# Another ending, four tiles of squares summed by TensorE, and new places for the interleaved work

## What is computed

```
x = x + mixer(layernorm(x))     # selective scan, 8 heads, state 64 x 128
x = x + ffn(layernorm(x))
x = x + attention(layernorm(x)) # 16 heads of width 8; its sequence axis is the batch of 8
x = x + ffn(layernorm(x))

# mixer, for each step t of 512
h = alpha * h + beta * Bx_prev + gamma * Bx_t
y_t = h . C_t
y = rmsnorm(y);  return y @ out_proj_w.T
```

## Time and profile before

| | us |
|---|---|
| median of 3 runs | 598.55 (597.16 to 598.97) |
| the profiled execution | 597.6 |
| its span, first to last instruction | 595.8 |
| busy: PE, DVE, ACT, POOL | 521.4, 470.9, 479.9, 433.6 |
| mean granted clock of PE | 0.968 |
| first scan, last scan start | 45.2, 523.9 |

### The profile page before, as it was taken

One profiled execution on the slowest core, in us unless ns is written; L12 is line 12 of the kernel. 1 busy time (PEld: TensorE's weight loads), 2 busy tenths in 40 slices (PEclk: granted clock), 3 DMA queues, 4 the chain that ended last, 5 costly groups with the idle time before them and its releaser, 6 DMA issues. The chain is left out here.

```text
span 595.8 us, 12817 instructions
## 1 busy us (share of the span) xinstructions
PE 521.4 (88%) x3932; PEld 435.3 (73%) x3932; DVE 470.9 (79%) x1093; ACT 479.9 (81%) x1477; POOL 433.6 (73%) x568
## 2 busy tenths in 40 slices
PE   4979999999999889899999898999999787879187
PEld 4867888888887777688887777788777665756085
DVE  5665577677767999997758999997559999954994
ACT  3799999999998987789998869699999889853101
POOL 7447777888778696977778786877768886954742
PEclk9989999999999999999999999999999999998669
DMA  8832122222111111133211121232211211000001
GB/s 191 234 101 64 59 77 98 60 81 89 49 59 61 60 50 35 61 95 96 60 38 59 61 61 54 66 96 95 72 50 39 69 62 65 21 19 2 0 1 36
DMA packets 52302, 39.35 MB, mean 66 GB/s; under 512 B 7302, under 2 KB 48011, under 8 KB 52235
## 3 DMA queue, kind: packets, MB, share of 16 engines
q1 hardware_dynamic: 45898, 35.39, 20.2%
q10 hardware_dynamic: 6336, 3.15, 1.8%
HBM read 33.44 MB, written 4.46 MB: 64 GB/s over the span
## 5 line engine op out<-in xcount | busy, mean ns | idle before, releaser
L937 ACT ACTIVATE turned<-ps,sct 128x128 f32<-128x128 f32 x376 | 110.2, 446 | 0.0
L922 ACT ACTIVATE turned<-ps,sct 128x128 f32<-128x128 f32 x368 | 102.9, 433 | 5.1 <-issue 4.3
L1282 DVE TENSOR_TENSOR_SCAN lmat<-arow,band 128x512 f32<-128x512 f32 x64 | 86.0, 1349 | 3.6 <-POOL band L651 3.6
L630 POOL TENSOR_TENSOR cn<-turned 128x256 f32<-128x256 f32 x64 | 54.9, 858 | 39.9 <-ACT turned L937 39.9
L1816 PE MATMUL ps<-cT,bT 128*128 128x128 f32 x512 | 71.4, 283 | 8.6 <-DVE state L1321 6.3
L1290 DVE TENSOR_TENSOR mmat<-ps,lmat 128x512 f32<-128x512 f32 x64 | 43.9, 686 | 44.0 <-PE ps L1816 43.8
L1816 PEld LDWEIGHTS ps<-cT,bT 128*128 128x128 f32 x512 | 64.1, 193 | 15.7 <-issue 14.5
L630 POOL TENSOR_TENSOR bn<-turned 128x256 f32<-128x256 f32 x64 | 51.9, 811 | 28.5 <-PE ps L1848 16.9
L828 ACT ACTIVATE area<-ps 128x256 f32<-128x256 f32 (+1 forms) x68 | 34.8, 568 | 39.9 <-PE ps L2049 14.3
L1721 PE MATMUL ps<-w_sel_hi,xt_hi 128*128 128x512 f32 x128 | 59.5, 465 | 1.6 <-ACT turned L937 1.6
L1848 PE MATMUL ps<-wu,bn 128*128 128x128 f32 x384 | 53.7, 283 | 3.5 <-DVE mmat L1290 3.4
(11 more groups left out here) (272 smaller groups left out, 1408.3 us busy)
## 6 DMA issues: line engine op xcount, KB each, us to landing
arow<-alpha_rows SPq DMA_DIRECT2D x32, 512.0 KB, 3.8
drow<-decay_rows SPq DMA_DIRECT2D x64, 128.0 KB, 3.0
area<-in_L_attn_a_x_dram SPq DMA_DIRECT2D x4, 512.0 KB, 6.6
xT_rows<-turned SPq DMA_DIRECT2D x4, 512.0 KB, 5.4
xt<-xT_rows SPq DMA_DIRECT2D x32, 64.0 KB, 2.5
area<-in_L_attn_a_x_dram ACTq DMA_DIRECT2D x6, 256.0 KB, 3.1
out_dram<-area ACTq DMA_DIRECT2D x6, 256.0 KB, 2.5
area<-L_attn_a_sel_proj_w_dram SPq DMA_DIRECT2D x2, 512.0 KB, 6.8
```

Of the source, the lines that this page charges most:

```text
L630: pool.tensor_tensor(out[:, 0], zc[:, 0], zs[:, 1], ALU.subtract)
L922: last = act.activation(dst[h][:, N * q:N * q + N], bank(BK_B)[:, N * q:N * q + N], ACT.Copy, scale=scalars(c, k)[:, at + HH * h + q:at + ...
L937: last = act.activation(dst[h][:, N * q:N * q + N], bank(BK_C)[:, N * q:N * q + N], ACT.Copy, scale=scalars(c, k)[:, at + HH * h + q:at + ...
L1282: dve.tensor_tensor_scan(lmat[h], arow[i2][:, HH * P * h:HH * P * (h + 1)], band[h], 0.0, ALU.mult, ALU.add).then_inc(l_dve, 1)
```

## The change

- **Squares.** For tiles 3 to 6 of every chunk `y_square` writes the squares in place order, `y_sum` is left out, and `project_out` sums the four blocks by four products with the column of ones into one bank column, where it was one product. `ysq` has two buffers now, by the tile's parity.
- **Places and orders.** All positions of `PLACE` are new, and so are the orders of `step` on POOL, ACT, DVE and PE.
- **Values.** `f_hvals` also writes the values with the row inside, (h, d, r), to `vals_er`, which lies in the buffer of chunk 2's x; so it waits for that chunk's stores. Rows 4 to 7 are weighed in this layout, and DVE sums the 8 rows of each by a reduction (`sum_values`); PE then only transposes them (`turn_row`). Rows 2 and 3 are folded from 8 blocks to 4 on POOL. Rows 0 and 1 stay.
- **Warming.** PE turns the identity ahead of the last tile's `project_out` (after y and after its squares), at three points ahead of the first values' sums (8 turns each), once between rows 0 and 1, and 8 turns in each of pairs 2 and 3.
- **Banks and order in the tail.** Pairs have other PSUM banks for their outputs, so the biases go in earlier. `attended` and `norm_of` alternate, and pairs 2 and 3 are turned and multiplied one after the other.

The diff, cut:

```diff
+SQUARES_ON_PE = (3, 4, 5, 6)
+def sums_done(c, b):
+    return (NB - len(SQUARES_ON_PE)) * c + len([q for q in range(b + 1) if q not in SQUARES_ON_PE])
...
-        ysq = sb("ysq", [P, 4 * P])
+        ysq_both = sb("ysq", [P, 2, 4 * P])
...
+        vals_er = area[:, 3072:4096].rearrange("p (e r) -> p e r", r=NB)
...
-        o_bank = [bank(BK_C), bank(BK_Y), bank(BK_C), bank(BK_Y)]
-        ffn_bank = [bank(BK_F0), bank(BK_M), bank(BK_F1), bank(BK_T)]
+        o_bank = [bank(BK_C), bank(BK_Y), bank(BK_F0), bank(BK_M)]
+        ffn_bank = [bank(BK_C), bank(BK_Y), bank(BK_F1), bank(BK_T)]
...
-                elif k < 0:
+                else:
                     scalars_ready(pool, c, k)
...
                     if ok(k, 1):
-                        band_of(c, k)
-                    at_span(pieces, c, k, 0, 0.583, first)
...
+                    if ok(k + 1, 1):
+                        band_of(c, k + 1)
...
+            def fold(s):
+                pool.wait_ge(tg, TG["v", s])
+                tick(pool.tensor_tensor(wide[s][:, 0:512], wide[s][:, 0:512], wide[s][:, 512:1024], ALU.add), ("a", s))
             values_of(2)
+            fold(2)
             values_of(3)
+            fold(3)
...
             def y_square(c, b):
-                after(act, q_dve, tile)
-                act.activation(ysq[:].rearrange("p (t j) -> p j t", j=4), yT[b % 2].rearrange("p (j t) -> p j t", j=4), ACT.Square)
+                after(act, o_pe, tile - 1)
+                own = ysq_both[:, b % 2]
+                if b in SQUARES_ON_PE:
+                    act.activation(own, yT[b % 2], ACT.Square).then_inc(ysq_act, 1)
+                else:
+                    act.activation(own.rearrange("p (t j) -> p j t", j=4), yT[b % 2].rearrange("p (j t) -> p j t", j=4),
+                                   ACT.Square).then_inc(ysq_act, 1)
...
             def f_hvals(c, p):
+                evac(vals_last[:, pair(p), :], rows)
+                for g in range(2):
+                    act.wait_ge(rows_free[g], 16 * NC)
+                evac(vals_er[:, :, pair(p)].rearrange("p e s -> p s e"), rows).then_inc(ha[p], 1)
...
             def y_sum(c, b):
+                if b in SQUARES_ON_PE:
+                    return
...
+            def sum_values(s):
+                if s in (4, 5):
+                    dve.wait_ge(tg, TG["v", s])
+                else:
+                    dve.wait_ge(tv, TV["v", s])
+                end_tick(dve.tensor_reduce(xn[:, s], wide[s].rearrange("p (e r) -> p e r", r=NB), AX.X, ALU.add), ("r", s))
...
             values_of(6)
             values_of(7)
-            fold(6, 512, "v", "a")
-            fold(7, 512, "v", "a")
-            fold(6, 256, "a", "h")
-            fold(7, 256, "a", "h")
+            sum_values(4)
+            sum_values(5)
+            sum_values(6)
             attended(0)
+            sum_values(7)
             attended(1)
             norm_of(0)
+            attended(2)
             norm_of(1)
-            attended(2)
             attended(3)
+            norm_of(2)
             add_to_x(0, ffn_bank[0], "F", "af")
             add_to_x(1, ffn_bank[1], "F", "af")
-            norm_of(2)
             norm_of(3)
...
             def project_out(c, b, more):
+                if in_ending(c) and b == NB - 1:
+                    for signal, count in ((y_dve, UNITS * NC), (ysq_act, NT)):
+                        pe.wait_ge(signal, count)
+                        keep_warm(WARM_LAST, BK_T)
...
+                if b in SQUARES_ON_PE:
+                    for j in range(4):
+                        last = pe.matmul(bank(BK_M)[:, D:D + 1], ysq_both[:, b % 2, P * j:P * j + P], ones[:, 0:1], start=(j == 0), stop=(j == 3))
...
+            for name in ("sum", "rec", "w"):
+                pe.wait_ge(tv, TV[name, 0])
+                keep_warm(WARM_VALUES, BK_C)
             add_rows(0, 0, NB)
+            pe.wait_ge(tv, TV["sub", 1])
+            keep_warm(WARM_LAST, BK_C)
             end_tick(add_rows(0, 1, NB), ("acc", 0))
-            add_rows(1, 2, NB)
-            end_tick(add_rows(1, 3, NB), ("acc", 1))
+            add_rows(1, 2, NB // 2)
+            end_tick(add_rows(1, 3, NB // 2), ("acc", 1))
...
-            add_rows(2, 4, NB)
-            end_tick(add_rows(2, 5, NB), ("acc", 2))
-            add_rows(3, 6, 2)
-            end_tick(add_rows(3, 7, 2), ("acc", 3))
+            for p in (2, 3):
+                turn_row(p, 2 * p)
+                keep_warm(WARM_ROWS, BK_T)
+                end_tick(turn_row(p, 2 * p + 1), ("acc", p))
+                out_of(p)
```

More of the change, by code:

```diff
@@ L1018, in f_hvals @@
                 act.wait_ge(hp[p], HEAD_P["KV"])
[L1019 removed]
+                rows = kv_bank[p].rearrange("p (s e) -> p s e", s=2)[:, :, D:2 * D]
+                evac(vals_last[:, pair(p), :], rows)
+                for g in range(2):
+                    act.wait_ge(rows_free[g], 16 * NC)
+                evac(vals_er[:, :, pair(p)].rearrange("p e s -> p s e"), rows).then_inc(ha[p], 1)
             def f_hrow(c, p):
@@ L1141, in _ @@
             exp_of(1)
-            turned_out("acc", 0, 0)
-            turned_out("acc", 1, 0)
-            turned_out("acc", 2, 0)
-            turned_out("acc", 3, 0)
+            for p in range(4):
+                turned_out("acc", p, 0)
             for p in range(4):
@@ L1858, in project_out @@
                     pe.matmul(bank(BK_M)[:, 0:D], yT[b % 2][:, P * j:P * j + P], w_out[:, j], start=(j == 0), stop=(j == 3))
-                pe.matmul(bank(BK_M)[:, D:D + 1], ysum[:], ones[:, 0:1], start=True, stop=True).then_inc(o_pe, 1)
+                if b in SQUARES_ON_PE:
+                    for j in range(4):
+                        last = pe.matmul(bank(BK_M)[:, D:D + 1], ysq_both[:, b % 2, P * j:P * j + P], ones[:, 0:1], start=(j == 0), stop=(j == 3))
+                else:
+                    last = pe.matmul(bank(BK_M)[:, D:D + 1], ysum[:], ones[:, 0:1], start=True, stop=True)
+                last.then_inc(o_pe, 1)
             def f_free(c, use):
@@ L1992, in step @@
                         project_b(c, k + 2)
-                    at_span(pieces, c, k, 0.45, 0.65, first)
                     if ok(k):
                         scores(c, k)
-                    at_span(pieces, c, k, 0.65, 0.75, first)
+                    at_span(pieces, c, k, 0.375, 0.542, first)
                     if ok(k + 2, 1):
                         project_c(c, k + 2)
-                    at_span(pieces, c, k, 0.75, 0.9, first)
+                    at_span(pieces, c, k, 0.542, 0.75, first)
                     if ok(k + 1):
                         turn_b(c, k + 1)
-                    at_span(pieces, c, k, 0.9, 1, first)
+                    at_span(pieces, c, k, 0.75, 0.833, first)
+                    if ok(k):
+                        outputs(c, k, not first or k >= FIRST_INTER)
+                    at_span(pieces, c, k, 0.833, 1, first)
                 else:
@@ L2005, in step @@
                         states(c, k - 1)
-                    if ok(k - 1):
-                        outputs(c, k - 1, not first or k - 1 >= FIRST_INTER)
-                    at_span(pieces, c, k, 0, 0.158, first)
                     if ok(k):
                         turn_c(c, k)
-                    at_span(pieces, c, k, 0.158, 0.263, first)
+                    at_span(pieces, c, k, 0, 0.147, first)
+                    if ok(k - 3):
+                        project_out(c, (k - 3) // 2, not (last and (k - 3) // 2 >= NB - 2))
+                    at_span(pieces, c, k, 0.147, 0.529, first)
                     if ok(k + 2, 1):
                         project_b(c, k + 2)
-                    at_span(pieces, c, k, 0.263, 0.316, first)
-                    if ok(k - 3):
-                        project_out(c, (k - 3) // 2, not (last and (k - 3) // 2 >= NB - 2))
-                    at_span(pieces, c, k, 0.316, 0.868, first)
+                    at_span(pieces, c, k, 0.529, 0.618, first)
                     if ok(k):
                         scores(c, k)
-                    at_span(pieces, c, k, 0.868, 0.921, first)
+                    at_span(pieces, c, k, 0.618, 0.824, first)
                     if ok(k + 2, 1):
                         project_c(c, k + 2)
+                    at_span(pieces, c, k, 0.824, 0.882, first)
                     if ok(k + 1):
                         turn_b(c, k + 1)
-                    at_span(pieces, c, k, 0.921, 1, first)
+                    at_span(pieces, c, k, 0.882, 1, first)
             def operands_ready():
@@ L2101, in _ @@
             ffn_of(1)
-            turn_pair(2)
-            turn_pair(3)
-            ffn_of(2)
-            ffn_of(3)
+            for p in (2, 3):
+                turn_pair(p)
+                ffn_of(p)
 _INS = ["L0_attn_a_x", "L0_attn_a_in_proj_w", "L0_attn_a_sel_proj_w", "L0_attn_a_out_proj_w", "L0_attn_a_A_log",
```

188 lines of the change are left out of this document (96 added, 92 removed), and 69 rows, old and new, of tables (PLACE, TV).

## The result

The changed kernel takes 607.75 us in the median (605.44 to 609.54), before 598.69 beside it: 1.016 of it, 95% interval 1.0127 to 1.0193. The forecast was 585.0 us, in 577.5 to 593.5. The profiled execution of the changed kernel is its fastest, 605.44 us (span 603.7); the span grew by 7.9 us.

The account below looks back on a forecast made before the run. ACT paced chunk 0, DVE the attention stage, PE and ACT units 14-15, waits the ending. Gains 5.4 + 1.0 + 0 + 0 + 5 + 2 = 13.4 us took 597.6 to 584.2, median 585.0 us; range 577.5 to 593.5.

Parts of the forecast that it names:

- the squares: Loop: sums of tiles 3 to 6 leave DVE and ACT writes squares plainly; 5.4 + 1.0 us won.
- the ending: After the last scan, some 72 us: head 5 us and tail 2 us won.
- the order: Loop: each engine's new step order is nearly the old one, cut elsewhere; 0 us, bounds -5 and +4.
- What bounds the kernel: Chunk 0: ACT, PE just behind; units 6 to 13 from chunk 1: DVE; units 14 and 15: PE and ACT.
- ACT's 1.0 us: Unit 14 of chunks 1 and 2: plainly written squares save ACT 2 x 0.5 us.
- 9 x 0.60: Chunks 1 to 3, where DVE is full: nine DVE sums removed, 0.60 us each, 5.4 us won.
- the cover: PE's side: 6 more passes per tile cost 0.65 us, fitting PE's free 1.5 us in the attention stage.
- Chunk 0, taken as 0: Chunk 0's four pairs: PE rises to some 12.2 us, ACT falls to 11.4; 0 us, bounds -2.0 and +1.4.
- The head: Start of the ending: last pair's norm 3.6 us sooner, idle 2.9 us gone, less costs; 5 us won, bounds 0 and 7.
- The tail: Last scores to last add: DVE's chain replaces PE's passes, with warming and POOL folds; 2 us won, bounds -1 and 4.
- PE as the pace: Rival: PE paces every tile, 10.4 us added and the loop's 6.4 not shown; 602 us, chance 0.05.
- Orders and places win by themselves: Rival: new orders and places fill DVE's idle time around the attention; 580 us, chance 0.16.

Follow-up runs that it names:

- a1: The kernel before with only the squares of tiles 3 to 6 summed on PE: 601.92 us, ratio 1.004 to 1.011.
- a4: The changed kernel with no squares on PE, all tiles summed by DVE: 610.73 us, ratio 1.017 to 1.025.
- a3: The kernel before with squares on PE and the new ending, old orders and places: 598.30 us, ratio 0.998 to 1.003.
- a2: The kernel before with the new ending alone, old orders and places, no squares on PE: 593.52 us, ratio 0.992 to 0.996.
- e1: Kernel before with the new ending alone, plus 12 PE turns ahead of unit 11's scores in chunks 1 and 2: 595.08 us, ratio 0.991 to 0.997.
- f1: Kernel before with new ending, PE squares only for tiles 3 to 5 of chunks 1 to 3, 8 turns before unit 11's scores (chunks 1, 2); repeat run: 594.01 us.
- e2: The kernel before with the new ending but without its new warming turns: 598.95 us, ratio 0.998 to 1.003.
- b4: The changed kernel with DVE's y_sum moved back behind the weighing of scores: 608.86 us, ratio 1.013 to 1.022.
- b2: The changed kernel with the old places for the head's pieces only: 604.42 us, ratio 1.007 to 1.015.

## Why the prediction was wrong

By the medians the 22.7 us between forecast and result are three sizes: the squares 11.2 (6.4 to win, 4.8 lost), orders and places 9.5, the ending 3.3 (7 forecast, 3.7 won); their sum of 24.0 is over by about what the kernel before was faster on the chip of a1 to a4 (597.26 for 598.69). With the order at its 0 the kernel would still have been outside the range, at a3's 598.3; the order made it slower than before.

**What bounds the kernel** was read rightly stage by stage, but units 14-15 too lightly. "The pair of units 14 and 15 is bound by PE and ACT together" stood there, and in the sum I let ACT's 1.0 us count there and forgot PE's passes.

**The squares**, 5.4 + 1.0 + 0 forecast, measured 0 between single profiled loops without a fall, and 4.8 us lost in the median of a3 against a2. Two steps failed. The first is the 9 x 0.60: six of the nine sums gave 0.1 to 0.9 us a pair and three gave 0.0 to 0.1, since the scan behind them met a POOL sum and took 0.55 longer; by pairs of e1 and f1 some 3.2 us are won for the 5.4. The second is the cover. Passes were costed where DVE is full; those of the later tiles land in units 14 to 1, where PE is nearly full, and e1 to f1 give 3.3 us back in units 14-15. Chunk 0, taken as 0, lost 0.7 us in units 12-13 (12.11 in a3 for 11.38), where PE was the pace. The plain square was right, 0.63 us. The loss in the median beyond that stays open: it is there at equal mean clock, and the one profiled execution of a3 is its fastest.

**The order**, "I take 0, bounds -5 and +4", measured +9.5 (a3 to the changed kernel), and is the step by which the kernel came out slower than before. No bound from rows stood behind +4: it was 0.15 us for each of 30 pairs, a guess. Inside it: x_high 2.0 us in chunk 0's pairs, a wait for a load in front of ACT's work where ACT sets the pace, of which I had named the move and not asked when the load lands; the head's places 3.3 us by the medians; y_sum 0 in this order; PE's outputs at most a gain, 2.4 us by the medians. The rest, some 6 us, is argued and not shown: by elimination it lies with the attention's places and cuts.

**The head**, 5 us forecast, measured 1.0: from the last scan to the last scores 32.9 us (535.0 to 567.84), 33.8 before (523.9 to 557.77). The wait for pair 2's add went, 3.6 us, as worked out. But 2.9 came ahead of it, between the last scan and the last output. Behind the last pair's first norm only 0.2 was won, for the 2.9 of the idle time before 550.66: 2.0 went as DVE's second norm met the POOL product that had been moved ahead. Of that product I counted the gain and not whom it shuts out, though I did so for the fold. And a2, with the old places, is at its last scores 31.5 us after its last scan (523.9 to 555.35), less than the changed kernel's 32.9: the earlier pieces bought nothing that the new ending with the old places did not.

**The tail**, 2 us forecast, measured 2.2: last scores to last add 33.6 us (567.84 to 601.45), 35.8 before. DVE's subtraction beside POOL's second product was held for 0.6 (0.4 taken). But I put the gain down to DVE's chain in place of PE's; e2 shows that without the turns nothing of it is left (36.2 us in its tail; 34.4 in a2).

**The rivals.** Slower than before had 0.04 and one mechanism, PE as the pace, which alone had 0.05: the chances did not agree. "Orders and places win by themselves" had 0.16, and its mirror image, that they lose, none, though bounds of -5 and +4 allow both.

## What to carry to other kernels

A table of places that was made for one order of steps says nothing under another: an order and its places are one change, and where no row prices them their range has two sides of at least the size of their stages. An edit that relieves the engine that sets the pace of one stage has to be followed with its work into the next stage, and work pulled into a full loop from an ending with idle time is paid at the loop's price. The largest new wait in a profile need not cost anything: b4 took 27 us of it away and gained nothing, while three waits of 0.45 to 0.8 us in front of ACT, where it sets the pace, cost 2.0. An instruction taken off a full engine pays only if the next one doesn't start into a neighbour's lock (the scan of 1.76 us for 1.21). And one profiled execution of a kernel is one draw: a late load or a fall of the clock in it is no property of the change until it shows in others.

## What the runs showed of the hardware

PE's low clock came in the middle of the loop too. In seven kernels (before, changed, a1 to a4, b2) there were sixteen falls in chunks 1 to 3: each began beside or within 2.3 us behind a pause of PE of 1.2 to 3.5 us, and PE then ran at 0.50 for 3.4 to 6.8 us. A pause need not bring one: the same seven executions have 75 pauses of 1.15 us and more there, and b4's has 14, up to 2.60 us, without a fall. With twelve turns in each of the two pauses of 2.0 us e1 had no fall, where five of six such pauses without turns had one. A fall of 3.4 us cost 0.8 us where DVE was the full engine (a2 to e1). The Trainium skill's "TensorE: Matmul & The Clock Gate" (The two states you'll see) calls the low clock the default that activity releases; the trace agrees, and shows that it can cost a full loop too.

Two DVE tensor_scalar instructions of 128x128 took 2.63 us together, 0.61 five us before: the second ran 2.37 us for 0.34, beside a POOL product of 2.37 us that had started 0.08 us ahead of it. The Trainium skill's "SBUF — State Buffer" (Who interferes with whom) names tensor_scalar among the VectorE operations that can shut GpSimd out and be shut out by it for a whole instruction, and says that a reduction never is; the trace agrees in the one, and DVE's row sums of the tail (1.2 us each, beside POOL's products) in the other.

A DVE scan took 1.76 us for 1.21 when it started 0.25 us behind a POOL sum of 0.92 us (f1 and e1, once in each of chunks 1 to 3).

A load of 24 KB (`sct`) landed 1.7 to 1.8 us after its issue in the median, and in 14 of the 20 profiled executions at least one in chunks 1 to 3 took 3.0 to 3.8 us.
